# A graph network kernel on one core: five units of the sorted list per step instead of four, and one comparison for their one-hots

## The reference

```python
h = relu(layernorm(x))
# filter layer
f = (softplus(edge_attr @ W1 + b1) - log 2) @ W2 + b2
x = x + segment_sum(h[dst] * f, src)       # taken from dst, summed at src
# two relational convolutions with 8 edge types over x[src], mean per (dst, type)
h = relu(layernorm(x)); x = x + rgcn2(relu(rgcn1(h)))
```

## Time and profile before

| | |
|---|---|
| median of 3 runs | 7135.0 us (7131.79 to 7145.11) |
| the profiled execution | 7149.4 us, its span 7147.6 us |
| preparation | 0 to 154 us |
| sorting steps, from the first scatter | 171 to 1466 us |
| adding steps | 1473 to 2707 us |
| table and two convolutions | 2707 to 7148 us |
| busy share of the span | PE 61%, DVE 53%, ACT 41%, POOL 75% |

### The profile page before, as it was taken

The page is one execution under the profiler, slowest core; times in us unless marked ns, Lnnn a source line. Parts: engine busy times, 40 slices in busy tenths (PEclk is TensorE's granted clock), DMA queues, the critical chain, the costliest instruction groups (busy, mean ns, idle before and its releaser), DMA issues. The chain is left out here.

```text
span 7147.6 us, 113836 instructions
## 1 busy us (share of the span) xinstructions
PE 4359.0 (61%) x28573; PEld 3531.3 (49%) x28573; DVE 3819.8 (53%) x11981; ACT 2911.5 (41%) x7788; POOL 5383.4 (75%) x5304
## 2 busy tenths in 40 slices
PE   2888888888888887645555555555444444444444
PEld 1666666667777773444444444444333333333333
DVE  8888888868777877645555555555211111111111
ACT  2666666654444446523333333333222222222222
POOL 6777777778888885577777777777677777777777
PEclk6999999999999998756666666666555555555555
DMA  3766666589998988634444443333222222222222
GB/s 107 188 183 182 181 181 162 149 173 190 188 189 186 192 166 273 209 89 104 106 106 106 105 105 105 106 105 103 67 55 56 56 56 56 56 56 56 56 56 54
DMA packets 688258, 879.21 MB, mean 123 GB/s; under 512 B 132110, under 2 KB 512426, under 8 KB 687277
## 3 DMA queue, kind: packets, MB, share of 16 engines
q1 hardware_dynamic: 446088, 530.23, 26.9%
q0 software_dynamic: 238864, 340.26, 21.9%
q10 hardware_dynamic: 2634, 1.21, 0.1%
HBM read 615.41 MB, written 255.76 MB: 122 GB/s over the span
## 5 line engine op out<-in xcount | busy, mean ns | idle before, releaser
L1907 POOL DMA_INDIRECT got<-table_dram,cidx x3322 | 3154.0, 949 | 1057.3 <-issue 996.9
L1956 PE MATMUL bank<-got,share 128*128 128x128 f32 x6656 | 1632.7, 422 | 1856.0 <-DMA got<-table_dram,cidx 1855.5
L1956 PEld LDWEIGHTS bank<-got,share 128*128 128x128 f32 x6656 | 1400.6, 311 | 2010.3 <-DMA got<-table_dram,cidx 2009.7
L1536 POOL DMA_INDIRECT msg_dram<-total,idx x1008 | 986.7, 979 | 335.3 <-issue 281.1
L2010 ACT ACTIVATE share<-cto_node,etcol 128x128 f32<-128x128 bf16 x3328 | 1071.1, 393 | 354.0 <-DVE cto_node L2101 318.4
L1551 POOL DMA_INDIRECT acc_dram<-total,idx x653 | 1035.7, 1586 | 206.5 <-issue 194.6
L2000 ACT ACTIVATE cidx<-srccol 128x4 int32<-128x4 f32 x832 | 169.5, 205 | 2395.2 <-PE bank L1956 2381.6
L303 DVE SCALAR_TENSOR_TENSOR xs<-bank,mask_hi,xs 128x128 f32 x416 | 146.2, 351 | 1690.0 <-PE bank L1956 1690.0
L1129 PEld LDWEIGHTS bank<-w,soft 128*128 128x128 f32 x3328 | 446.1, 195 | 56.7 <-issue 41.5
L1129 PE MATMUL bank<-w,soft 128*128 128x128 f32 x3328 | 447.1, 278 | 0.0
L1120 PE MATMUL bank<-edges_t,w 128*128 128x512 f32 x832 | 428.9, 597 | 2.4 <-DVE soft L1360 2.4
(11 more groups left out here) (262 smaller groups left out, 7877.8 us busy)
## 6 DMA issues: line engine op xcount, KB each, us to landing
edges<-in_edge_attr SPq DMA_DIRECT2D x415, 256.0 KB
unit<-msg_dram SPq DMA_DIRECT2D x616, 129.0 KB
clow<-rows_dram SPq DMA_DIRECT2D x416, 128.0 KB
got<-table_dram,cidx POOLq DMA_INDIRECT x3322
table_dram<-made SPq DMA_DIRECT2D x98, 512.0 KB, 5.0
table_dram<-umade SPq DMA_DIRECT2D x98, 512.0 KB, 3.0
low<-rows_dram SPq DMA_DIRECT2D x164, 256.0 KB
win<-split_dram SPq DMA_DIRECT2D x416, 96.0 KB
```

What stands on the lines that cost most here:

```text
L1536: pool.indirect_dma_start(g.msg_dram[:, :], bass.IndirectOffsetOnAxis(ap=idx[k][:, j:j + 1], axis=0), total[k][:, j, :], None).then_inc(s_ ...
L1907: pool.indirect_dma_start(got[k][:, j, :], None, g.table_dram[which][:, :], bass.IndirectOffsetOnAxis(ap=idx[k][:, j:j + 1], axis=0)).then ...
L1956: ins = nc.tensor.matmul(window[k], share[k][:, j, :], got[ka][:, j, :], start=j == 0, stop=j == TG - 1)
```

## The change

Five units per step instead of four. NA becomes 272 and the adding steps 144; 134 of these take units; the main units are 544 for 504, which need two banks where one sufficed. The unit buffers are three instead of four, and so are `split` and `h` of the preparation, to make room. The five comparisons become an add of the block offset (`key`) and one comparison over all five units, at the end of DVE's step. Adds two, three and four stand together ahead of `soften`. The fifth result lies in free columns of bank 6, beside the totals, which brings two waits to TensorE: the totals wait for the first add, and the reduction waits for ACT's copy of `total` of the same step.

```diff
-UNITS = 4
+UNITS = 5
...
 # prepare
-    NSP = 4
-    NH = 4
+    NSP = 3
+    NH = 3
...
-            nc.tensor.matmul(g.bank[7][:, 0:NMAIN], g.ones3[:, :], ended, start=True, stop=True).then_inc(s_counted, 1)
+            nc.tensor.matmul(g.bank[3][:, 0:NMAIN - 512], g.ones3[:, :], ended[:, 512:], start=True, stop=True)
+            nc.tensor.matmul(g.bank[7][:, :], g.ones3[:, :], ended[:, 0:512], start=True, stop=True).then_inc(s_counted, 1)
...
-                chain(v.tensor_copy(so.unit_blk[:, 0:NMAIN], g.bank[7][:, 0:NMAIN]))
-                chain(v.tensor_scalar(so.unit_off[:, 0:NMAIN], g.bank[7][:, 0:NMAIN], -float(P), None, ALU.mult))
+                for blocks, c0, c1 in ((g.bank[7], 0, 512), (g.bank[3], 512, NMAIN)):
+                    chain(v.tensor_copy(so.unit_blk[:, c0:c1], blocks[:, 0:c1 - c0]))
+                    chain(v.tensor_scalar(so.unit_off[:, c0:c1], blocks[:, 0:c1 - c0], -float(P), None, ALU.mult))
...
 # filter_layer
-    NU = 4
+    NU = 3
...
-        reduced = [bank_r[:, m * P:(m + 1) * P] for m in range(UNITS)]
+        reduced = [bank_c[1][:, HALF * (F + 1):HALF * (F + 1) + P]] + [bank_r[:, m * P:(m + 1) * P] for m in range(UNITS - 1)]
+        key = sb("key", [P, UNITS, UNIT // P, 1])
...
 # TensorE, ahead of the totals
                         need(pe, s_totc, s.at(3))
+                        if windows.own and s.live(UNIT_LAG + 3, NA + g.NSET, NA):
+                            need(pe, s_added, b.at(UNIT_LAG + 3) * UNITS + 1)
...
 # TensorE, ahead of the reduction
                         need(pe, s_added, b.at(lag) * UNITS)
+                        need(pe, s_totc, s.at(3) + 1)
...
 # VectorE, a step of adding
                     if ready:
                         add_unit(b, 2)
+                    if ready:
+                        add_unit(b, 3)
+                        add_unit(b, 4)
                     if s.live(1, NG, start):
                         soften(s, False)
-                    if ready:
-                        add_unit(b, 3)
...
+                        need(dve, s_unit_hot, b.at(lag))
-                        for m in range(UNITS):
-                            ins = v.scalar_tensor_tensor(unit_hot[b.slot(2, lag)][:, m, :, :],
-                                                         unit[b.slot(NU, lag)][:, m, :, F:F + 1].to_broadcast([P, UNIT // P, P]),
-                                                         so.unit_off[:, bass.ds(b.at(lag) * UNITS + m, 1)],
-                                                         so.iota_f[:, :].unsqueeze(1).to_broadcast([P, UNIT // P, P]),
-                                                         ALU.add, ALU.is_equal)
-                        ins.then_inc(s_unit_hot, 1)
+                        v.tensor_tensor(key[:, :, :, 0], unit[b.slot(NU, lag)][:, :, :, F],
+                                        so.unit_off[:, bass.ds(b.at(lag) * UNITS, UNITS)].unsqueeze(2).to_broadcast([P, UNITS, UNIT // P]),
+                                        ALU.add).then_inc(s_key, 1)
...
 # at the end of the step, behind the message and the counts
+                    if keyed:
+                        lag = UNIT_LAG + 1
+                        need(dve, s_key, b.at(lag) + 1)
+                        v.tensor_tensor(unit_hot[b.slot(2, lag)][:, :, :, :].rearrange("p m k q -> p (m k) q"),
+                                        key[:, :, :, 0].rearrange("p m k -> p (m k)").unsqueeze(2).to_broadcast([P, UNITS * (UNIT // P), P]),
+                                        so.iota_f[:, :].unsqueeze(1).to_broadcast([P, UNITS * (UNIT // P), P]),
+                                        ALU.is_equal).then_inc(s_unit_hot, 1)
```

More of the change, by code:

```diff
@@ L148, in __init__ @@
         self.NFIX = self.NU - self.NMAIN
-        assert self.NBX <= self.NFIX <= P and self.NMAIN <= 512 and self.NA >= 16
+        assert self.NBX <= self.NFIX <= P and 512 < self.NMAIN <= 1024 and self.NA >= 16
         self.acc_dram = [nc.dram_tensor(f"acc_dram{j}", [self.NACC, F], F32).ap() for j in range(TG)]
@@ L350, in prepare @@
         idf = [ids[k].bitcast(F32) for k in range(3)]
-        spare = sb("spare", [P, max(EQ, g.NT)], I32)
+        spare = sb("spare", [P, max(EQ, g.NT, 2 * g.NTA)], I32)
         idt = spare[0:QP, 0:EQ]
@@ L370, in prepare @@
         scaled = sb("scaled", [F, F])
-        digits = [wide[1][:, 0:EQ // 2].bitcast(BF16)[:, k * NTA:(k + 1) * NTA] for k in range(2)]
+        digits = [wide[1][:, 0:EQ // 2].bitcast(BF16)[:, 0:NTA], sb("low_digit", [P, NTA], BF16)[:, :]]
         pick = wide[1][:, EQ // 2:].bitcast(F32)
@@ L914, in filter_layer @@
         edges = [sb(f"edges{k}", [P, TG, F]) for k in range(NE)]
-        rows = [sb(f"rows{k}", [2, GE], BF16) for k in range(NE)]
         low = [sb(f"low{k}", [P, 2, GE], BF16) for k in range(NE)]
@@ L922, in filter_layer @@
         chunk_split = pieces[2].bitcast(BF16)[:, 0:CB * 3 * F].rearrange("p (b k f) -> p b k f", k=3, f=F)
+        rows = [unit[2][0:2, :, :, :].rearrange("p m k f -> p (m k f)").bitcast(BF16)[:, k * GE:(k + 1) * GE] for k in range(NE)]
         place = sb("place", [P, TG])
@@ L956, in filter_layer @@
         s_unit_hot = sem("f_unit_hot")
+        s_key = sem("f_key")
         s_red = sem("f_red")
@@ L1468, in step @@
                                         ALU.max).then_inc(s_idx, 1)
-                    if windows.own and s.live(UNIT_LAG + 1, NA + g.NSET, NA):
+                    keyed = windows.own and s.live(UNIT_LAG + 1, NA + g.NSET, NA)
+                    if keyed:
                         lag = UNIT_LAG + 1
```

## The result

The changed kernel takes 7191.0 us in the median (7181.7 to 7197.8, 4 runs) beside 7134.2 us for the kernel before (7131.8 to 7145.1): a ratio of 1.0076, interval 1.0064 to 1.0089. It is slower by 57 us. The forecast was 7145.5; the time came out where the fourth rival put it (7189). The profiled execution's own time is 7192.2 us, its span 7190.3.

A forecast was written before the change was run, and what follows sets the result against it. The prediction took POOL's indirect DMAs to bound sorting and adding. Its terms, -48.5 for moved steps, +12.5 for preparation and +46.5 for a loop through SP's loads, sum to +10.5 us: 7145.5 us, range 7096 to 7205.

The forecast's parts named there:

- the fourth rival: Adding steps: edge loads queue on busy DMA engines and land 3.71 us late, P = 8.33, 7189 us; chance 0.25.
- What bounds the kernel: Sorting and adding: POOL's unbroken line of indirect DMAs sets both step periods, 5.138 and 7.563 us.
- Moved steps and preparation: Twenty steps go from adding to sorting, -48.5 us; fewer `split` and `h` buffers and more columns lengthen preparation, +12.5 us.
- The comparison's own time: DVE in an adding step: one comparison of 1280 elements takes 1.48 us, replacing four that issue in 1.67.
- The loop: Adding: three unit buffers tie unit sums, SP's loads, edges and transposes into a two-step loop, 2P = 12.95 + L; +46.5 us.
- P: Period of one adding step under the closed buffer loop: 8.0 us, bounds 7.66 to 8.33, against 7.563 before.
- The landing L: Adding: time from the end of the edges' issue until they land, taken as 3.05 us between 2.36 and 3.71.
- the first link: Adding: from the end of the unit sums (reduction) to SP's first unit load, 0.75 us.
- the last: Adding, on PE: from the transposes to the end of the unit sums (reduction), 6.8 us.
- The two waits: PE in adding: totals find the first add done in time; the reduction begins 0.7 us after ACT's copy, formerly 1.2 before.
- POOL stays the bound: Adding: DVE, PE and SP's shortest round fit into POOL's 7.56 us; in all -36.0 us, 7099 us; chance 0.22.
- The adds ahead of the softplus: DVE in adding: two adds behind another, 0.6 to 0.67 us with register load; with the fifth add +0.9, hidden under POOL.

The follow-up runs named there:

- experiment 4: Kernel before with three buffers instead of four for `split` and `h`, nothing else changed: 7142.8 us, ratio 1.0011.
- experiment 7: Kernel before with its four comparisons of 256 columns replaced by keys and one comparison of 1024 columns, still four units: 7174.9 us, ratio 1.0052.
- experiment 5: Changed kernel with four unit buffers and the one comparison over five units cut into five, one per unit: 7120.6 us, ratio 0.9979.
- experiment 8: Kernel before with three unit buffers, and the unit sums also waiting for ACT's copy of the totals: 7151.5 us, ratio 1.0022.
- Experiment 6: Changed kernel with four unit buffers, five comparison pieces, the fourth add behind the softplus and the fifth behind `same`: 7149.6 us, ratio 1.0018.
- experiment 9: Changed kernel with four unit buffers and five comparison pieces, with marks, indices and keys moved between DVE's adds: 7130.5 us.
- experiment 1: Changed kernel with four unit buffers instead of three, small tiles moved to make room: 7129.0 us, ratio 0.9989.

## Why the prediction was right and wrong

- **What bounds the kernel:** right. POOL's two lines of scatters set both stages of the kernel before; sorting behaved exactly as forecast (80 more at 0.977 + 0.305 us).
- **Moved steps and preparation:** right. 10.2 us for 12.5; experiment 4 gives 8.0 for the 9.2 of the buffers.
- **The comparison's own time:** right, and the wrong question. 1.48 us was forecast and is measured. That it cost "nothing while POOL leads" is the step that failed: the instruction holds up POOL, the very engine that led. In the kernel before, that alone is 37 us (experiment 7). The scatters of 1660 ns stand for 573 x 0.074 = 42 us of POOL's time in the changed kernel; the loop hides most of it.
- **The loop:** right as a mechanism, since a fourth buffer or the edges ahead of the units bring back 62 and 52 us. Its size was wrong: P came out 8.36 (16.71 for two steps) for 8.0, 131 x 0.36 = 47 us, about the 45 by which adding is over its forecast. The landing L was taken at 3.05, the middle between 2.36 and 3.71, and that was near: 3.26 in the mean. The rest is 0.26 in the first link, taken at its shortest although SP is often late by itself, and 0.22 in the last, most of it the lower clock behind late edges, which no term held. With the right L alone the sum would have given P = 8.10 and 7159.
- **Rival 4's figure:** 7189 was met, but by luck. It put P = 8.33 down to landings of 3.71 each; such landings are single ones, and three links together make the 8.36. The fit that the prediction took from the Trainium skill (DMA: Bandwidth & Descriptors, Anatomy of one DMA) stands in a section on DMAs that GpSimd issues, and these are issued by SP. Its 2.6 us with the issue included is 2.2 without the 0.43 of the issue, not 2.4, and lies under every landing here.
- **The two waits:** the one for the first add hardly shows in the changed kernel (1.9 us in 6 waits of 950 us), as forecast; in experiment 5 it is 98.9 us in 104 waits. The one for ACT's copy was told as a delay, but the 6.8 us of the loop hold no term for it, rightly: 0.4 us in the changed kernel, and experiment 8 finds it free.
- **"POOL stays the bound", 7099:** refuted even without the loop. With four buffers the kernel takes 7129, and 27 us of the distance are the longer scatters (573 x 0.047). With five pieces as well 7121 remain. A step lasts some 7.8 us there (121 in 950 us), POOL alone would need 7.55, and a quiet round of DVE takes 7.67; the adds in a row (0.77 apart, 0.6 to 0.67 forecast) are part of that. What holds the step in that kernel was not separated.
- **The adds ahead of the softplus:** priced as DVE time only. Experiment 6 shows what they are good for: 29 us against a loop of 8.02.

The forecast's sum failed in one term, P. Two errors of some 40 us each that I had not separated (the loop's size, and the scatters' length) did not add up, because the longer of two parallel bounds sets the step.

## What to carry to other kernels

Cost a long VectorE instruction with two SBUF operands also to GpSimd: every indirect DMA that starts inside it is longer by what is left of it less 0.12 us, so if GpSimd is the bound, several short instructions may beat one that is faster by itself; whether they do depends on where the scatters fall (experiment 9). When a buffer is taken away, write out the loop that closes over it and take every link at its mean in a busy stretch, not at its shortest; then test with one buffer more. Measure the links over many turns: the one turn first looked at here had a landing of 4.90, the mean is 3.26. And where two bounds lie side by side, removing one shows only the distance to the other, so remove both (7191 to 7129 to 7121).

## What the runs showed of the hardware

- A scatter of 128 rows takes 1.55 us undisturbed, and when it starts during a DVE instruction with two SBUF operands it is longer by the rest of that instruction less 0.12 us: up to 1.33 us (2879 ns at most in experiment 1). If it starts up to 0.027 us behind such an instruction, it is not longer, and DVE's instruction is, by up to 0.07. Five instructions that follow each other every 0.34 us count as five in experiment 5 and mostly as one in experiment 9.
- Edge loads of 256 KB landed 3.16 us after their issue in the mean of the 97 that PE waited for (2.43 to 5.16) at 88% busy DMA engines, beside the quiet 2.36.
- TensorE's granted clock fell to 1.2 GHz fifteen times in 950 us of the changed kernel, each time with a wait of 1.95 to 2.98 us for edges, and the transposes to the end of the sums then took 8.24 us for 6.73.
- A DVE add that reads its target from a register and waits for the add ahead comes every 0.77 us though it takes 0.29; two small instructions with waits of their own between them (0.33 + 0.16) moved it to 1.31. Why they don't hide in the gap was not tried apart.
